# A graph layer's edge loop on one core: VectorE's z waits for the msg_lo two back instead of the one right in front of it

## What is computed

```python
h = jnp.maximum(_layernorm(x), 0.0)
edge_emb = edge_attr @ W_edge + b_edge
msg = jax.nn.relu(h[src] + edge_emb)
aggr = jax.ops.segment_sum(msg, dst, num_segments=N)
u = (1.0 + eps) * h + aggr
u = gelu(layer_norm(u @ W1 + b1, g1, be1))
u = gelu(layer_norm(u @ W2 + b2, g2, be2))
u = layer_norm(h + u, gA, bA)
m = gelu(u @ M1) @ M2
return x + layer_norm(u + m, gB, bB)
```

## Time and profile before

| | |
|---|---|
| median of three runs | 490.02 us |
| profiled execution, its own time | 489.55 us |
| its span, first to last instruction | 487.5 us |
| TensorE busy | 460.0 us (94%) |
| VectorE busy | 393.1 us (81%), 563 instructions |
| ScalarE busy | 310.5 us (64%) |
| GpSimd busy | 267.0 us (55%) |
| DMA moved | 85.27 MB, mean 175 GB/s |

### The profile page before, as it was taken

One profiled execution on the slowest core, in us unless ns is written; L12 is line 12 of the kernel. 1 busy time (PEld: TensorE's weight loads), 2 busy tenths in 40 slices (PEclk: granted clock), 3 DMA queues, 4 the chain that ended last, 5 costly groups with the idle time before them and its releaser, 6 DMA issues.

```text
span 487.5 us, 7358 instructions
## 1 busy us (share of the span) xinstructions
PE 460.0 (94%) x1927; PEld 340.2 (70%) x1928; DVE 393.1 (81%) x563; ACT 310.5 (64%) x586; POOL 267.0 (55%) x299
## 2 busy tenths in 40 slices
PE   6629999999999999999899999999999999999994
PEld 2205666666666666666678888888888898888883
DVE  6898899999999999899847777789989755752575
ACT  4847788898999999999716555567665672033000
POOL 4867777777777777774015443346553551410342
PEclk9969999999999999999999999999999999999999
DMA  7968899788888878775094232535511240220122
GB/s 266 337 220 271 293 301 316 246 254 248 251 266 268 255 251 247 245 243 158 3 327 149 86 108 87 178 102 172 170 47 65 55 120 0 87 86 0 45 90 82
DMA packets 31430, 85.27 MB, mean 175 GB/s; under 512 B 4609, under 2 KB 4945, under 8 KB 31378
## 3 DMA queue, kind: packets, MB, share of 16 engines
q0 software_dynamic: 12560, 41.17, 27.5%
q1 hardware_dynamic: 18818, 43.51, 26.2%
HBM read 72.08 MB, written 5.24 MB: 159 GB/s over the span
## 4 chain that ended last, share of the span: by engine, by line
PE 37%; DVE 26%; issue 10%; ACT 9%; POOL 6%; DMA 6%; ACTq 2%; DVEq 0%; SPq 0%; POOLq 0%
DVE msg_lo L1167 11%; DVE z L1161 9%; PE ps_u L1386 8%; PE ps_u L1388 8%; PE ps_u L1387 8%; PE ps_t L1386 3%; PE ps_t L1388 3%; PE ps_t L1387 3%; POOL rows L630 3%; ACT msg_hi L837 3%; ACT apart L760 3%; PE ps_t L1539 2%; DMA rows<-gather_table,src_idx 2%; DMA w_raw<-in_W 2%; DMA rows<-in_x,src_idx 1%
## 5 line engine op out<-in xcount | busy, mean ns | idle before, releaser
L630 POOL DMA_INDIRECT rows<-gather_table,src_idx x153 | 152.6, 997 | 46.5 <-issue 46.5
L648 POOL TENSOR_TENSOR var_eps<-mv,eps_t 128x1 f32<-128x1 f32 x40 | 20.6, 515 | 137.8 <-ACT squares L909 80.2
L837 ACT ACTIVATE msg_hi<-z 128x1024 fp32r<-128x1024 f32 (+1 forms) x79 | 82.7, 1047 | 19.9 <-DVE z L1161 19.6
L1167 DVE SCALAR_TENSOR_TENSOR msg_lo<-z,msg_hi 128x1024 fp32r<-128x1024 f32 (+1 forms) x79 | 95.1, 1206 | 0.0
L1161 DVE TENSOR_TENSOR z<-ps_u,rows 128x1024 f32<-128x1024 f32 (+1 forms) x53 | 64.2, 1211 | 9.8 <-PE ps_u L1404 3.1
L1404 PE MATMUL ps_u<-we_raw,attr_raw 128*128 128x512 f32 x134 | 68.0, 617 | 3.5 <-DMA attr_raw<-in_attr_t 3.1
L1386 PE MATMUL ps_u<-w_hi,lhs_lo 128*128 128x512 f32 x160 | 64.5, 403 | 1.6 <-DVE lhs_lo L1230 1.6
L1388 PE MATMUL ps_u<-w_hi,lhs_hi 128*128 128x512 f32 x160 | 62.6, 392 | 0.0
L1387 PE MATMUL ps_u<-w_lo,lhs_hi 128*128 128x512 f32 x160 | 62.3, 390 | 0.0
L1422 PE MATMUL ps_t<-msg_hi,onehot 128*128 128x512 f32 x149 | 58.5, 393 | 0.0
L1422 PE MATMUL ps_t<-msg_lo,onehot 128*128 128x512 f32 x149 | 58.5, 393 | 0.0
(11 more groups left out here) (181 smaller groups left out, 1031.1 us busy)
## 6 DMA issues: line engine op xcount, KB each, us to landing
attr_raw<-in_attr_t SPq DMA_DIRECT2D x20, 512.0 KB, 5.4
w_raw<-in_W SPq DMA_DIRECT2D x24, 256.0 KB, 2.9
tile_in<-mid SPq DMA_DIRECT2D x10, 512.0 KB, 3.6
res<-in_x SPq DMA_DIRECT2D x20, 256.0 KB, 2.7
xin<-in_x SPq DMA_DIRECT2D x5, 512.0 KB, 5.2
out<-work SPq DMA_DIRECT2D x10, 256.0 KB, 2.0
rows<-gather_table,src_idx POOLq DMA_INDIRECT x153, 4.2
gather_table<-tab SPq DMA_DIRECT2D x4, 512.0 KB, 4.4
```

The source lines that it names most:

```text
L630: g.indirect_dma_start(rows[:, group.r, e % TPG, :], None, gather_table[:, :], bass.IndirectOffsetOnAxis(src_idx[:, e:e + 1].bitcast(u32), ...
L837: a.activation(pair(msg_hi, g, p), summed(g, p), ACT.Relu).then_inc(msg_hi_done, 1)
L1167: v.scalar_tensor_tensor(pair(msg_lo, g, p), summed(g, p), 0.0, pair(msg_hi, g, p).bitcast(f32), ALU.max, ALU.subtract).then_inc(msg_lo_do ...
```

## The change

In add_rows the wait for msg_lo_done asks for one less. The z of pair n = 2 gr + p writes into place n mod 4 of the ring z, which the msg_lo of pair n - 4 was the last to read. That msg_lo is number n - 3 in the count. Before, the wait asked for n - 2, the msg_lo of pair n - 3. Nothing else changes.

```diff
                 dve.wait_ge(emb_done[p], g.gr + 1)
-                if 2 * g.gr + p >= 3:
-                    dve.wait_ge(msg_lo_done, 2 * g.gr + p - 2)
+                if 2 * g.gr + p >= 4:
+                    dve.wait_ge(msg_lo_done, 2 * g.gr + p - 3)
                 v.tensor_tensor(summed(g, p), embedded(g, p),
```

## The result

The changed kernel takes 518.56 us in the median of four runs (516.43 to 520.77), against 490.14 for the kernel before: a ratio of 1.057, 95% interval 1.054 to 1.060. It is 28.4 us slower, far outside the range of 488.3 to 504.0, and close to the 516 of rival 3. The profiled execution took 516.82 us and has a span of 514.7.

What follows compares the result with a forecast made beforehand. TensorE was taken as the bound now, with GpSimd's held gathers bounding the loop after the change: +7.4 us in the loop less 2.0 behind the last z, net +5.4, giving 495.4 us; range 488.3 to 504.

Steps and rivals of the forecast that it cites:

- rival 3: GpSimd issues 0.06 us behind a msg_lo are held too: 12.0 us a four, 516 us; chance 0.10.
- the largest gain: Edge loop: however fast VectorE becomes, it gives back at most TensorE's idle time, 0.57 + 1.29 = 1.9 us.
- VectorE's part: z starts 1.13 us behind msg_lo instead of 1.35; plain step 2.27 instead of 2.49, unhindered 9.6 us a four.
- Rival 2: No change: z still starts 1.35 us after msg_lo, or VectorE's gain and GpSimd's loss cancel; 490.0 us, chance 0.15.
- What holds the gathers: A GpSimd gather coming up during msg_lo, which has two SBUF inputs, is held and ends 2.03 us behind msg_lo's start.
- 2.33 (0.06 behind a msg_lo, where no row decides, taken as free): GpSimd schedule: the issue after a held one starts unheld; only a later issue loses 0.78 us.
- The pace of GpSimd: GpSimd's gathers set the edge loop's pace at 10.80 us per four pairs, own range 10.5 to 11.3.
- The closed loop through landings of 5.5 us: Issue-to-issue loop of landing, z to msg_lo, hold and next issue: 3.0 us a pair, 12.0 a four.
- The tail: Behind the last z the end comes sooner, as TensorE's queue of scatter products shrinks: 2.0 us credited.
- the last half pair: Behind the last z, without TensorE's queue: z 0.69 us, msg_hi, msg_lo and two products, 2.8 us in all.
- Stretch z9 to z78: From the z at 57.05 us to the last at 235.92, 17.25 fours: 186.3 us at 10.80 each, 7.4 more.

Runs made afterwards that it cites:

- the experiments with one input: msg_lo made a reduction reading z alone, msg_hi's subtraction left out: 489.01 us in the changed kernel, 489.19 us in the kernel before.
- plain copies: Changed kernel with each GpSimd gather replaced by a plain copy of one tile, without indices: 489.66 us.
- the copies: Changed kernel with one, three or four one-element copies before z in three of four pairs: 532.91, 524.86 and 506.68 us.
- the kernel with one copy: Changed kernel with one single-element copy on VectorE before z in three of four pairs: 532.91 us, ratio 1.085.

## Why the prediction was wrong

**What bounds the kernel, and the largest gain: right.** TensorE was full, and taking the collision away gave 1.7 us with the new wait and 1.4 with the old, both inside the bound of 1.9. A gain from the short step alone is not shown.

**VectorE's part: right.** 1.13 us from msg_lo to z and a plain step of 2.27, as worked out from the earlier trace rows. Rival 2 is out: the wait did cost 0.22 us each time, which the page "VectorE: DVE Perf Modes" of the Trainium skill, section "The DRAIN you can't avoid", would not have had.

**What holds the gathers: right.** Two operands in SBUF on VectorE and a read of SBUF on GpSimd, as the Trainium skill's page "SBUF — State Buffer", section "Who interferes with whom", says; the experiments with one input and with plain copies took away one half each, and the holds went. The second took more than the read, as said there. That held issues end 2.03 us behind the start of msg_lo stood too, apart from those that run on into attr_lo (2.43 and more).

**The step that failed: "2.33 (0.06 behind a msg_lo, where no row decides, taken as free)".** 21 of 21 such gathers were held, by 1.02 us each. The prediction had named the place where no row decides and priced the other answer as rival 3, 12.0 us a four and 516 us; measured 11.95 and 516.82 for the profiled execution. It gave this 0.10 and the other the whole forecast, and cut the range short of it. Nothing in its rows favoured "free": they put the edge only between 0.15 before and 0.22 behind, and 0.06 behind is near the middle of that. The reading of 0.15 was itself off: 29 ordinary issues of the kernel before start 0.11 to 0.14 us before a msg_lo. Half and half would have been the least, with a range up to 516. And by the table under the copies, 0.06 is held whether the z in front waited (from 0.034 on) or ran on. The schedule then was also too kind in form: it let a gather at 2.33 through and so started the next fresh, where in truth a hold produces the next hold.

**The pace of GpSimd: right engine, 10.80 against 11.95 a four.** The excess accounts for it: 8 x 1.2525 = 10.02, and 40.4 us over the 19 fours of all gathers are 2.1 more, 12.1 a four for the gathers; the z, which had some rows in hand at the start, ran at 11.95. The closed loop through landings of 5.5 us, by which rival 3 arrived at its 12.0, is not what set it: GpSimd waited for nobody, and landings had a median of 3.9 us between 100 and 230. Rival 3's working was right only in its first half, and that its number came out so near is in part luck.

**The tail: -2.0 us credited, 0.4 measured.** The next stage's first transposes start at 269.04, 5.04 us behind the last z, against 5.43. The estimate of 2.8 us for the last half pair supposed that the scatter products in front of it were done. But a msg_lo trails its z by two pairs, so three msg_lo stood behind the last z on VectorE in any case. The timeline of VectorE of the kernel after:

```profile
264.00 0.68 DVE L1161 TENSOR_TENSOR z<-ps_u,rows 128x512 f32<-128x512 f32 x1
264.61 2.95 DVE L1167 SCALAR_TENSOR_TENSOR msg_lo<-z,msg_hi 128x1024 fp32r<-128x1024 f32 x3
```

They last until 267.56, and the products behind them start the next stage 1.5 us later. This was to be read from the order on VectorE.

**The sum by terms.** Stretch z9 to z78: 206.11 - 178.87 = +27.2 us, forecast +7.4. Start of it: 57.89 - 57.05 = +0.8, forecast 0. Tail: -0.4, forecast -2.0. The node part behind: 245.66 against 246.15, -0.5. Together +27.2 = 514.7 - 487.5. Nearly all the error is in the first term.

**Left open.** No run tells why a z that ran on brings the edge forward, from 0.03 us behind msg_lo to 0.12 before it. Nor is that forward edge one line: with a z that ran on, issues 0.112 to 0.124 us before msg_lo were held in 26 of 38 cases and those 0.104 to 0.111 before, which are nearer, in none of 14. No run had the short step and a z that waits, so how the 28 us divide between the two effects of the wait is not measured.

## What to carry to other kernels

When two engines share a resource and run at nearly the same period, read their phase, not only their load: here a wait of 0.22 us on an engine that was not the bound kept the step at 2.49 us, and 0.22 less set off a chain of holds that costs 28. A wait can also do more than take time: with the step back at 2.51 us but no wait, the kernel still lost 16. Before you shorten one of two such engines' steps, compute where the other one's next instruction will start, once for the free case and once for the held one; if a place falls where no row decides, give both answers a like chance. And an excess that is hidden has a limit that can be read: how far the last transfer is ahead of its user.

## What was not expected of the hardware

- Whether the instruction in front had waited moves the start of the hold: none of 193 issues was held from 0.20 us before to 0.028 behind a msg_lo whose z had waited, and 145 of 145 from 0.067 before to 0.13 behind one whose z had run on.
- The hold goes both ways: an issue that comes first is free and lengthens msg_lo, from 1.21 us to 1.26 when it starts with msg_lo (kernel after, 185.57) and to 1.28 when it starts 0.03 us behind.
- Two instructions with two SBUF operands back to back can hold a gather through both: in the kernel with one copy, issues at 0.01 us behind a msg_lo with attr_lo behind it took 2.48 us where others took 2.02. In the kernel after, at 0.07 behind, one of nine did (2.43 us).
- Copies of one element cost VectorE 0.06 us each in the step (2.27, 2.33, 2.45, 2.51 for none, one, three, four).
- Chips can differ by more than the change: the kernel before took 490.1 to 490.7 us in three comparisons and 535.08 us on one other chip; with plain copies in place of the gathers that chip gave 489.66. It is not the holds: with one input in msg_lo no issue was long there and the kernel took 534.19. So it goes with the gathers; what in them, no run tells.
